# Attention steps of a gated attention + expert-choice layer: values move to the second quarter of a step, output transposes to the fourth, and the finish of a batch to the end of VectorE's step

## The reference

```python
def _L0_xattn_ref(q, k, v, mask, Wq, bq, Wk, bk, Wv, bv):       # 16 heads of 16
    Qh = (q @ Wq + bq).reshape(B, S, H, dh)                      # Kh, Vh alike
    scores = jnp.einsum('bqhd,bkhd->bhqk', Qh, Kh) / jnp.sqrt(jnp.float32(10.0))
    scores = jnp.where(mask[:, None, None, :] == 0, jnp.float32(-1000000000.0), scores)
    probs = jax.nn.softmax(scores, axis=-1)
    return jnp.einsum('bhqk,bkhd->bqhd', probs, Vh).reshape(B, S, D)

def _L0_ffn_ref(x, Wg, W1, W2, W3):                              # 8 experts, each takes its top 1024 tokens
    scores = (x_flat @ Wg.T).T
    top_vals, token_idx = jax.lax.top_k(scores, capacity)
    token_w = jax.nn.softmax(top_vals, axis=-1)
    xg = x_flat[token_idx]
    h = jax.nn.silu(jnp.einsum('eic,ehc->eih', xg, W1)) * jnp.einsum('eic,ehc->eih', xg, W3)
    y = jnp.einsum('eih,ech->eic', h, W2) * token_w[..., None]
    out = jnp.zeros_like(x_flat).at[token_idx.reshape(-1)].add(y.reshape(-1, c))

x = x + jnp.tanh(g_xattn[0]) * _L0_xattn_ref(_layernorm(x), ctx_1024, ctx_1024, mask, ...)
x = x + jnp.tanh(g_ffn[0]) * _L0_ffn_ref(_layernorm(x), ...)
```

## Time and profile before

| | |
|---|---|
| median of three executions | 1028.93 us (1025.36 to 1029.19) |
| the profiled execution | 1030.7 us, of which its span 1029.0 us |
| TensorE busy | 814.6 us, 79% of the span |
| VectorE busy | 544.1 us, 53% |
| ScalarE busy | 474.1 us, 46% |
| GpSimd busy | 425.9 us, 41% |
| mean granted TensorE clock | 0.906 of full speed |

### The profile page before, as it was taken

How to read it: one execution, slowest core, us unless ns; L and a number is a source line. 1 busy time by engine, 2 the same in 40 slices (tenths; PEclk the granted TensorE clock), 3 DMA queues, 4 the chain that set the end, 5 groups by cost and what they waited for, 6 DMA issues and landing times. The chain is left out here.

```text
span 1029.0 us, 22168 instructions
## 1 busy us (share of the span) xinstructions
PE 814.6 (79%) x6988; PEld 624.8 (61%) x6988; DVE 544.1 (53%) x1416; ACT 474.1 (46%) x930; POOL 425.9 (41%) x790
## 2 busy tenths in 40 slices
PE   3588898889888988898887411148999999999995
PEld 1365666656665666566666311115878878878874
DVE  1457777677667766776677268795222222222220
ACT  2246666665666566656666400002344344344331
POOL 3334433433344334333431140032467566566524
PEclk9789999999899989998999755556999999999998
DMA  4875566866575658565662240011146245245223
GB/s 116 222 197 132 168 188 194 219 156 176 170 214 153 190 162 221 151 192 158 172 168 75 87 158 0 1 37 48 21 124 127 39 125 124 38 127 122 38 26 41
DMA packets 99258, 130.57 MB, mean 127 GB/s; under 512 B 12896, under 2 KB 62336, under 8 KB 99200
## 3 DMA queue, kind: packets, MB, share of 16 engines
q1 hardware_dynamic: 86912, 112.78, 39.4%
q0 software_dynamic: 12288, 17.05, 9.7%
HBM read 52.34 MB, written 26.49 MB: 77 GB/s over the span
## 5 line engine op out<-in xcount | busy, mean ns | idle before, releaser
L541 ACT ACTIVATE p_t<-b_ps 128x512 f32<-128x512 f32 x256 | 147.8, 587 | 54.2 <-PE b_ps L838 52.4
L684 DVE TENSOR_REDUCE m_sb<-a_ps 128x4 f32<-128x512 f32 x256 | 164.9, 676 | 14.8 <-PE a_ps L825 13.9
L1335 POOL DMA_INDIRECT out<-y,idx_add x64 | 100.1, 1564 | 88.4 <-ACT y L1377 68.3
L1462 DVE TENSOR_TENSOR hid<-act_h,bank 128x512 f32<-128x512 f32 x64 | 44.0, 688 | 147.1 <-PE bank L1506 115.4
L1526 PE MATMUL bank<-w,hid 128*128 128x256 f32 x512 | 116.4, 379 | 0.0
L825 PE MATMUL a_ps<-k_st,q_st 97*128 97x128 bf16 x1024 | 100.1, 221 | 18.7 <-DMA k_st<-k_part 13.9
L455 POOL TENSOR_TENSOR q_part<-q_rest,q_part 128x512 bf16<-128x512 f32 x32 | 36.9, 1154 | 182.0 <-ACT q_part L512 182.0
L1506 PE MATMUL bank<-x_hi,w_hi 128*128 128x512 f32 x256 | 103.3, 403 | 7.5 <-DVE hid L1462 6.0
L825 PEld LDWEIGHTS a_ps<-k_st,q_st 97*128 97x128 bf16 x1024 | 73.9, 98 | 52.4 <-issue 46.9
L1325 POOL DMA_INDIRECT xg<-rows_scratch,idx x64 | 61.3, 959 | 104.4 <-DVE idx L1175 70.7
L838 PE MATMUL b_ps<-q_st,k_st 99*128 99x128 bf16 x1024 | 100.3, 221 | 4.7 <-ACT p_t L541 4.7
(11 more groups left out here) (182 smaller groups left out, 1468.5 us busy)
## 6 DMA issues: line engine op xcount, KB each, us to landing
q_st<-q_part SPq DMA_DIRECT2D x96, 256.0 KB, 4.7
k_st<-k_part SPq DMA_DIRECT2D x96, 256.0 KB, 4.0
w<-in_w_t SPq DMA_DIRECT2D x24, 512.0 KB, 5.4
rows_scratch<-row SPq DMA_DIRECT2D x16, 528.0 KB, 4.1
x_in<-in_x SPq DMA_DIRECT2D x16, 512.0 KB, 4.7
c_t<-in_ctx_t SPq DMA_DIRECT2D x16, 512.0 KB, 4.8
x_res<-in_x SPq DMA_DIRECT2D x16, 512.0 KB, 3.9
out<-x SPq DMA_DIRECT2D x16, 512.0 KB, 3.1
```

Of the source, the lines that this page charges most:

```text
L541: act.activation(p_t[b.s % 2][:, 4 * q:4 * q + 4, :], b_ps[q % 2][:].rearrange("p (h s) -> p h s", s=P), ACT.Exp, scale=SCALE).then_inc(ex ...
L684: dve.tensor_reduce(m_sb[b.s % 2][:, 4 * q:4 * q + 4], a_ps[q % 2][:].rearrange("p (h s) -> p h s", s=P), AX_X, ALU.max).then_inc(max_done, 1)
L1335: pool.indirect_dma_start(out[:, :], bass.IndirectOffsetOnAxis(ap=idx_add[e.p][:, st:st + 1], axis=0), y[st][:], None, compute_op=ALU.add) ...
L1462: dve.tensor_tensor(hid[n // FT][:, n % FT, :], act_h[n % 2][:], h3_ps[:, 0:SPAN], ALU.mult).then_inc(hid_done, 1)
```

## The change

In the attention stage four things are written in another order. No instruction is added or removed.

TensorE: `values` of batch b-3 goes from quarter 2 to quarter 1, and with it `router` and `scores_back`, which also go one step later (steps 1 and 2 in place of 0 and 1). `out_back` of batch b-4 goes from quarter 2 to the end of quarter 3 (`OT_AT` = 3). `xn2_back` goes from quarter 0 to quarter 2 (`XT_AT` = 2), in the same steps.

ScalarE: `mid_q` and `mid_k` of half 0 go ahead of the second `exp`; `pv_copy`, `router_out` and `xt2_copy` go to the place right behind that `exp`.

VectorE: `finish` of batch b-4 goes behind the last `maximum` of the step, so that the next step's first `maximum` stands right behind it; `row_scores` goes from step 1 to step 2.

GpSimd's and SyncE's lists stay as they are.

```diff
@@ -57,7 +57,7 @@
-OT_AT = 2
+OT_AT, XT_AT = 3, 2
@@ -599,34 +599,32 @@
                 if b.j == 2:
                     hi_k(f, 0)
                 neg_hi(b.back(1))
-                if b.j == 0:
-                    xt2_copy(g.on(-3), 1)
-                if b.j == 3:
-                    xt2_copy(g.on(-2), 0)
                 if b.j == 2:
                     normalise2(g.on(-2), (0, 1))
                 if b.j == 3:
                     normalise(g.on(2), (0, 1))
                 exp(b.back(2), 0)
-                exp(b.back(2), 1)
                 if b.j == 1:
                     mid_q(f, 0)
                 if b.j == 2:
                     mid_k(f, 0)
+                exp(b.back(2), 1)
+                pv_copy(b.back(3))
+                if b.j == 1:
+                    router_out(g.on(-3))
+                if b.j == 3:
+                    xt2_copy(g.on(-2), 0)
                 if b.j == 0:
+                    xt2_copy(g.on(-3), 1)
                     xn_t_out(f, 1)
...
                 exp(b.back(2), 2)
-                pv_copy(b.back(3))
-                if b.j == 0:
-                    router_out(g.on(-3))
@@ -757,16 +755,15 @@
                 maximum(b, 1)
                 maximum(b, 2)
-                finish(b.back(4))
                 if b.j == 1:
                     rest_q(f, 1)
                 if b.j == 2:
                     make_k(f, 1)
+                    row_scores(b.group.on(-3))
                 if b.j == 3:
                     make_v(f, 1)
                 maximum(b, 3)
-                if b.j == 1:
-                    row_scores(b.group.on(-3))
+                finish(b.back(4))
@@ -918,24 +915,24 @@
                 for q in range(4):
                     scores(b, q)
-                    if q == OT_AT:
-                        out_back(b)
                     scores_t_(*((b.back(2), q - 1) if q else (b.back(3), 3)))
-                    if q == 2:
+                    if q == 1:
                         for i in range(4):
                             values(b.back(3), i)
-                        if b.j == 0:
+                        if b.j == 1:
                             router(g.on(-3), b)
-                        if b.j == 1:
+                        if b.j == 2:
                             scores_back(g.on(-3), b)
+                    if (b.j, q) == (3, XT_AT):
+                        xn2_back(g.on(-2), 0, (g, q, b.j))
+                    if (b.j, q) == (0, XT_AT):
+                        xn2_back(g.on(-3), 1, (g, q, b.j))
                     if q in (0, 2):
                         front(g.on(1), 2 * b.j + q // 2)
                     if q == 0:
                         max_t(b)
-                    if (b.j, q) == (3, 0):
-                        xn2_back(g.on(-2), 0, (g, q, b.j))
-                    if (b.j, q) == (0, 0):
-                        xn2_back(g.on(-3), 1, (g, q, b.j))
+                    if q == OT_AT:
+                        out_back(b)
```

More of the change, by code:

```diff
@@ L255, in attention @@
     O_USES = sorted([((j, OT_AT), "ot", j) for j in range(GB)]
-                    + [((3, 0), "xt", 0), ((0, 0), "xt", 1)])
+                    + [((3, XT_AT), "xt", 0), ((0, XT_AT), "xt", 1)])
     O_LAG = {("xt", 0): 2, ("xt", 1): 3}
@@ L621, in step @@
                     hi_k(f, 1)
-                if b.j == 2:
                     normalise2(g.on(-2), (2, 3))
@@ L884, in max_t @@
                         pe.wait_ge(f_free[1], 4)
-                    if b.j == 1 and g.ok:
+                    if b.j == 2 and g.ok:
                         pe.wait_ge(r_out, g.times(1, 1))
                         pe.sem_inc(passed, 1)
-                    if b.j == 2 and g.ok:
+                    if b.j == 3 and g.ok:
                         pe.wait_ge(st_out, g.times(1, 1))
```

## The result

The changed kernel took 1071.04 us (median of four executions, 1066.06 to 1071.53) against 1029.06 us of the kernel before beside it: ratio 1.0403, interval 1.0363 to 1.0444. It is 42 us slower. The forecast was 7.6 us slower.

The account below looks back on a forecast made before the run. The prediction took a 33.33 us loop through GpSimd's chain and the k_st transfer as the bound; 0.48 - 0.24 + 0.67 = +0.9 us a group, +11.8 us, less 4.2 for the clock: +7.6, 1036.5 us, range 1024 to 1052 us.

Parts of the forecast that it names:

- sign of a missed wait: A group well over 35 us at full clock would mean that the forecast had missed a wait.
- The ring through `mid_k`, GpSimd and the transfer: Attention stage: a 33.33 us loop through the engines, including GpSimd's layer norm, `rest_k`, `mid_k` and the k_st transfer, sets the group period.
- The first rival: TensorE's own work sets the period; without the two targeted waits 25 to 29 us go, 1000 to 1004 us; 14 in 100.
- worth exactly 0: Removing the `xn2_back` and `out_back` waits, 2.73 us a group, gains 0 while the k_st transfer is late.
- `mid_k` ahead of the exponential, 0.48 us a group: ScalarE: the exponential between the two `mid_k` makes the second `mid_k` and its transfer 0.48 us later a group.
- TensorE still fits beside the chain: Despite its stop, TensorE reaches step 0 about 0.6 us before the k_st transfer.
- TensorE would stop for 3.7 us at the head of step 3: Transposed scores wait for the second exponential, queued behind `mid_k`'s wait: 3.7 us in place of 0.88 + 1.51 + 1.22 us.
- Step 0, -0.24 us: `finish` ahead of the first maximum delays `scores`, but the router's products leave the step: -0.24 us a group.
- Step 1, +0.67 us: VectorE's list with `finish` starts the second query product 5.68 us into the step instead of 5.01: +0.67 us a group.
- `row_scores`, `router_out`: 0: Moving these costs 0, in the shade of the 3.7 us that `rest_k` had in hand behind GpSimd's chain.
- The clock, -4.2 us: TensorE's clock falls in most groups but mostly briefly: 0.5 us a group, 6.5 us, against 10.7 us before.
- The third rival: A long stop behind the second exponential drops the clock in every group: +26 us, 1055 us; 12 in 100.

Follow-up runs that it names:

- the other way: Changed kernel with the statistics of the next input put behind `neg_mid` on VectorE in step 1: 1044.54 us, ratio 1.0161.
- the first experiment: Changed kernel with `router` and `scores_back` ahead of `max_t` at the heads of steps 1 and 2, `router_out` and `row_scores` moved up: 1044.07 us, ratio 1.0154.

## Why the prediction was wrong

The sign was right, the size wrong: 7.6 us forecast, 42 measured, outside the range. The forecast's own sign of a missed wait came up: a group well over 35 us at full clock (36.51 us in the one from 275.50 on, with the clock at 1.00 from 276.00).

- **What bounds the kernel before: right.** The ring through `mid_k`, GpSimd and the transfer set the period: rearranging GpSimd's list alone gained 30 us. The first rival (the waits were the bound) fell: they are nearly gone in the changed kernel, and it is slower. That they are worth exactly 0 is not shown, since no run moved `xn2_back` and `out_back` alone.
- **`mid_k` ahead of the exponential, 0.48 us a group: right in the chain, with luck in the sum.** The rows show 0.46 (3.47 between the two `mid_k`, 3.01 before), and the part alone cost 6 us against 6.2. But in that run the clock falls in nearly every group and TensorE, not the transfer, comes last at step 0, so the forecast's remark that TensorE still fits beside the chain failed there by a few tenths of a microsecond. That TensorE would stop for 3.7 us at the head of step 3 is right for the part alone (3.6) and wrong for the whole change (1.35), where TensorE comes there later.
- **Step 0, -0.24 us: right where the clock doesn't fall in it** (5.34 to 5.39 us in six of the twelve groups, against 5.37), and by luck in its reason: I didn't count on `values` in the second quarter, which by my reading gives VectorE the time for `finish`. With `finish` last and `values` at its old place the step takes 7.12 us. In the other six groups it takes 5.9 to 6.9 us.
- **Step 1, +0.67 us: this step failed.** I put VectorE's list right, to within 0.4 us, and then wrote that this wait "hides the router's products and `values`, which stand in the same wait", and "`row_scores`, `router_out`: 0". `values` it did hide. The router's products it could not: they begin with a wait of their own for `neg_mid`, which stands behind `rest_q` in the very list that I added up. So they start when the wait should have ended, and they and the third quarter's `scores` and `scores_t_` come on top: 7.07 us on the mean in place of 5.68, 6.98 at full clock and 7.92 at worst. In my account of the move I followed what `router` costs TensorE (less than a microsecond) and not what it waits for. Taking that wait away gives back 27 us, or 26.5 by the other way, and adding it alone costs 26. That covers most of the 34 us between forecast and measurement: 1.4 us a group for the missed wait itself (18 us), and 0.4 us for the slower query product behind it (5 us), with the rest outside these two pieces.
- **The clock, -4.2 us: wrong in sign by my estimate.** It fell oftener than before (of the twelve windows from `mid_k` to `mid_k`, eleven have a mean clock of 0.96 or less, where five had one below 1.00 before), as the Trainium skill's rule in the forecast had it for every group ("TensorE: Matmul & The Clock Gate", section "HAM oscillation — how this bites in real kernels"). But it did not fall behind the exponential. In these twelve groups it falls thirteen times: six times in step 0, behind the wait at its head, four times in step 1 and three times in step 2. In step 0 that costs up to 1.6 us on the ring, in step 1 0.8 to 1.5 us for the query product and up to 0.9 ahead of it, in step 2 nothing that the pieces show. These excesses over the groups without a fall there add up to some 14 us, an estimate, against 6.5 forecast and 10.7 before. In the kernel before the forecast read the falls as coming after both waits of step 3; the row of one such group shows the clock down from 194.6 us on (0.51 to 198.0), and the second wait ended at 194.77, so it fell within that wait. The third rival was near in size (1055 us) and wrong in its mechanism, as the 6 us of the exponential alone show.

What stays open: how the other 15 us (1044.07 against 1029) divide between `finish`, the wait of `max_t` for `row_scores` that the first experiment brought in itself (18.0 us of TensorE's idle time in 400), and the clock. The parts don't add. A kernel in which `router` has a bank of its own, and so no wait of `m_free`, with the products in the change's place wasn't tried, nor was `values` early by itself.

## What to carry to other kernels

When a piece of work is moved in an in-order list, write down every semaphore that it waits for, not only its own length, and find the instruction that gives it in the other engine's list as it will be; a shared PSUM bank is such a wait even where the data have nothing to do with each other. A moved piece stops all that is behind it: 0.6 us of router products cost 26 us. Read more than one group: the group shown first here is the worst of twelve for the missed wait, and a sum worked out from it alone would come out 0.8 us a group too high. Look for the ring that sets the period first, and change the engine on it (here GpSimd's order, 30 us for two moved lines) before the waits that are longest in the bottleneck engine's list.

## What the runs showed of the hardware

The clock fell after shorter waits than any that I had counted on: in step 1 of one group of the changed kernel after waits of 0.96 and 0.97 us with `scores_t_` and 1.1 us of `values` between. In the group after 275.50 it did not fall after longer ones, of 2.46 us (for k_st) and 1.99 us (for `neg_mid`), so the length of a single wait doesn't tell. Windows of the changed kernel just before and in the fall of step 1, in a fall of step 0, in one of step 2, and over that group without a fall:

```profile
330.00:333.80 3.80, 1.95 (x42) 1.36 (x40) 3.38 (x14) 1.55 (x4) 0.00 (x0) 1.00 0.26 92
333.80:337.20 3.40, 3.32 (x26) 2.21 (x27) 1.32 (x3) 1.74 (x4) 1.15 (x1) 0.52 0.01 2
397.17:403.83 6.66, 6.62 (x81) 5.82 (x82) 3.55 (x7) 3.84 (x9) 2.98 (x15) 0.74 0.80 270
456.00:461.00 5.00, 5.00 (x32) 3.02 (x29) 2.35 (x6) 2.24 (x5) 3.13 (x8) 0.66 0.42 90
276.00:312.01 36.01, 28.87 (x357) 21.61 (x354) 26.31 (x60) 21.16 (x45) 13.41 (x38) 1.00 0.61 171
```

At 0.52, that is 1.2 GHz for nearly all of the second window, TensorE works without a pause on `router`, one quarter and the query product, so that the fall lies where the ring passes. The third window is a whole step 0, 6.66 us long at 0.74, where it takes 5.35 without a fall. The fourth lies in step 2, where TensorE isn't what the ring waits for, and the group that holds it takes 35.65 us, less than any other from the third on. So the price of a fall depends on where it lies.
